# Two long attentions of a one-core kernel: which engine turns and splits the probabilities, where VectorE's side work stands, and how the softmax denominators are added

## What is computed

```python
x = x + xattn0(LN(x), ctx, mask)      # 16 heads of 64, 64 queries x 6272 keys, masked softmax   <- first long attention
x = x + attn0(LN(x))                  # 16 heads of 8 over the 64 tokens, rotary, causal
x = x + moe0(LN(x))                   # 8 experts of width 512, top 2
x = x + xattn1(LN(x), ctx)            # o1 = x1 + attn(x1, ctx); then attn(o1, o1, x1)            <- second long attention
x = x + delta1(LN(x))                 # gated delta rule with convolutions and FIR branches
x = x + ffn1(LN(x))                   # weights rounded to 8 bits per column, values to 16 bits
```

## Time and profile before

| | |
|---|---|
| median of three timed runs | 424.36 us |
| profiled execution, in all | 426.19 us |
| its span, first to last instruction | 424.4 us |
| mean granted TensorE clock | 0.984 |
| first long attention, first score to last PV | 22.0 to 177.2 us |
| second long attention | 217.8 to 365.4 us |
| DMA queue of SP | 186,080 packets, 66.31 MB |

### The profile page before, as it was taken

How to read it: one execution, slowest core, us unless ns; L and a number is a source line. 1 busy time by engine, 2 the same in 40 slices (tenths; PEclk the granted TensorE clock), 3 DMA queues, 4 the chain that set the end, 5 groups by cost and what they waited for, 6 DMA issues and landing times.

```text
span 424.4 us, 12031 instructions
## 1 busy us (share of the span) xinstructions
PE 390.8 (92%) x4785; PEld 309.7 (73%) x4785; DVE 317.9 (75%) x872; ACT 287.3 (68%) x568; POOL 203.1 (48%) x128
## 2 busy tenths in 40 slices
PE   6888999999989999998997899899999999999885
PEld 3846777777767778887964677677777778888784
DVE  2598888888877877645669999998888878454534
ACT  3367888788887886546427798789899876352230
POOL 2267879879865551001001559888766550020000
PEclk9699999999999999999999999999999999999969
DMA  8779797989989988960004999999999999400000
GB/s 318 297 219 172 151 175 126 181 137 207 239 165 231 213 164 141 405 280 2 4 2 88 197 169 193 189 172 182 188 204 198 194 192 237 175 2 3 4 0 5
DMA packets 186426, 68.14 MB, mean 161 GB/s; under 512 B 181361, under 2 KB 181889, under 8 KB 185473
## 3 DMA queue, kind: packets, MB, share of 16 engines
q1 hardware_dynamic: 186080, 66.31, 76.7%
q10 hardware_dynamic: 288, 1.05, 0.7%
HBM read 21.90 MB, written 0.03 MB: 52 GB/s over the span
## 4 chain that ended last, share of the span: by engine, by line
PE 44%; DVE 28%; issue 8%; DMA 6%; ACT 6%; POOL 4%; SPq 3%; DVEq 0%; POOLq 0%; ACTq 0%
PE ps L497 13%; DVE probs L591 12%; PE ps L465 12%; DMA probsT<-halves 4%; PE ps L725 4%; DVE probsT L620 3%; POOL halves L567 2%; ACT probs L535 2%; DVE U L609 2%; PE ps L1137 2%; PE ps L477 2%; PE ps L1042 2%; DMA moe<-in_ctxT 2%; DVE den L604 1%; ACT halves L542 1%
## 5 line engine op out<-in xcount | busy, mean ns | idle before, releaser
L567 POOL TENSOR_TENSOR halves<-probs,halves 128x896 f16<-128x896 f32 x67 | 126.6, 1892 | 81.9 <-ACT halves L542 81.1
L465 PE MATMUL ps<-ctxT_parts,GT_parts 128*128 128x512 f16 (+1 forms) x672 | 145.4, 353 | 11.9 <-DVE negmax L591 10.0
L497 PE MATMUL ps<-ctxN,probsT 128*128 128x128 f16 x2352 | 149.4, 219 | 5.0 <-DMA probsT<-halves 3.5
L497 PEld LDWEIGHTS ps<-ctxN,probsT 128*128 128x128 f16 x2352 | 139.6, 98 | 18.7 <-DVE U L609 4.9
L535 ACT ACTIVATE probs<-probs,shifted 128x896 f32<-128x896 f32 x112 | 115.5, 1031 | 9.7 <-DVE shifted L596 9.7
L465 PEld LDWEIGHTS ps<-ctxT_parts,GT_parts 128*128 128x128 f16 x672 | 60.0, 98 | 64.3 <-DVE negmax L591 14.9
L542 ACT CAST halves<-probs 128x896 f16<-128x896 f32 x92 | 84.9, 922 | 0.1
L591 DVE CUSTOM_DVE_ANT_0 probs<-ps,maskb,negmax 128x896 f32<-128x896 f32 x56 | 67.4, 1204 | 1.2 <-POOL halves L567 0.7
L591 DVE CUSTOM_DVE_ANT_0 probs<-ps,zero,negmax 128x896 f32<-128x896 f32 x56 | 67.4, 1204 | 1.0 <-PE ps L465 0.8
L609 DVE SCALAR_TENSOR_TENSOR U<-U,alpha,ps 128x128 f32<-128x128 f32 x112 | 38.2, 341 | 32.3 <-PE ps L497 32.3
L532 ACT ACTIVATE alpha<-negmax 128x1 f32<-128x1 f32 x96 | 28.2, 294 | 42.4 <-DVE negmax L591 41.5
(11 more groups left out here) (347 smaller groups left out, 361.0 us busy)
## 6 DMA issues: line engine op xcount, KB each, us to landing
moe<-in_ctxT SPq DMA_DIRECT2D x7, 448.0 KB, 8.0
moe<-in_mask SPq DMA_DIRECT2D x6, 448.0 KB, 10.7
moe<-in_gateT SPq DMA_DIRECT2D x2, 1024.0 KB, 9.3
moe<-in_upT SPq DMA_DIRECT2D x2, 1024.0 KB, 11.2
moe<-in_downT SPq DMA_DIRECT2D x2, 1024.0 KB, 13.1
moe<-in_fir_long SPq DMA_DIRECT2D x1, 2048.0 KB, 10.4
probsT<-halves SPq DMA_TRANSPOSE x92, 4.5
wv<-in_wv SPq DMA_DIRECT2D x2, 512.0 KB, 5.3
```

The source lines that it names most:

```text
L465: ins = pe.matmul(ps[:, 2 * b + h, 0:width], GT_parts[:, g_part, r * P:(r + 1) * P], ctxT_parts[:, keys:keys + width], start=(g_part == 0 ...
L497: ins = pe.matmul(ps[:, bank, 0:D], probsT_parts[:, b, p_part, k * P:(k + 1) * P], ctxN_parts[:, at:at + D], start=(p_part == 0 and c_part ...
L567: eng.tensor_tensor(halves_of(L, n)[:, 1, :], probs[:, n % BUFS, :], halves_of(L, n)[:, 0, :], ALU.subtract).then_inc(lower_of(L, n)[0], 1)
```

## The change

TensorE's turns in the first attention: before, every fourth step (n % 4 = 3) and 53 to 55; now n % 4 = 3 only for 4 <= n < 32, and 51, 53, 54, 55 as before. Step 3 goes to GpSimd and the DMA; steps 35, 39, 43 and 47 go to VectorE (low half) and the DMA. In the second attention VectorE no longer makes the low halves of steps 0, 1, 3, 7 and 11; GpSimd does. `den` is updated once per chunk for all eight row tiles with two instructions on 128 x 8 (behind the maximum of index 13, 21, 29, 37, 45 and 53); only the last chunk is still added column by column. The weight maxima stand behind the projection of the first attention and the scales in the small attention; `keep_o1` moves from index 2 to 14. The mask of chunk 1 is made one low half earlier, and the eight rounding stages stand at every fourth step from 12 to 40.

```diff
+TURN_UNTIL, RAMP = 32, 12
         def on_pe(L, n):
-            return L == 0 and n % 4 == 3 or n >= STEPS - 3 or n == STEPS - 5
+            return L == 0 and n % 4 == 3 and 4 <= n < TURN_UNTIL or n >= STEPS - 3 or n == STEPS - 5
         def on_vector(L, n):
             if L == 0:
-                return n in (0, 2) or 4 <= n < 30 and n % 4 == 1 or n == STEPS - 4
-            return n % 4 == 3 or n in (0, 1, STEPS - 4)
+                return (n in (0, 2) or 4 <= n < 30 and n % 4 == 1 or n >= TURN_UNTIL and n % 4 == 3
+                        or n == STEPS - 4)
+            return n >= RAMP and n % 4 == 3 or n == STEPS - 4
...
             def add(n):
-                r = n % RT
-                dve.wait_ge(sem("exp_done"), base + n + 1)
-                if n >= RT:
+                r, c = n % RT, n // RT
+                if c == CH - 1:
+                    dve.wait_ge(sem("exp_done"), base + n + 1)
                     dve.wait_ge(sem("den_added"), base + n - RT + 1)
-                dve.tensor_scalar(den[:, r:r + 1], den[:, r:r + 1], alpha[:, n:n + 1], chunksum[:, n:n + 1],
-                                  ALU.mult, ALU.add).then_inc(sem("den_added"), 1)
+                    dve.tensor_scalar(den[:, r:r + 1], den[:, r:r + 1], alpha[:, n:n + 1], chunksum[:, n:n + 1],
+                                      ALU.mult, ALU.add).then_inc(sem("den_added"), 1)
+                elif r == RT - 1:
+                    tiles = slice(c * RT, (c + 1) * RT)
+                    dve.wait_ge(sem("exp_done"), base + n + 1)
+                    if c:
+                        dve.wait_ge(sem("den_added"), base + c * RT)
+                    dve.tensor_tensor(den[:], den[:], alpha[:, tiles], ALU.mult).then_inc(sem("den_added"), 1)
+                    dve.wait_ge(sem("den_added"), base + c * RT + 1)
+                    dve.tensor_tensor(den[:], den[:], chunksum[:, tiles], ALU.add).then_inc(sem("den_added"), RT - 1)
...
-                if n == 2:
+                if n == 0:
                     mask(1)
...
-                        if 12 <= n < 28 and n % 2 == 0:
-                            quantise_weights((n - 12) // 8, (n - 12) // 2 % 4)
+                        if 12 <= n < 44 and n % 4 == 0:
+                            quantise_weights((n - 12) // 16, (n - 12) // 4 % 4)
...
             project_dve(dve, 0)
+            loaded(dve, "ffn")
+            for i, w in enumerate((win, wout)):
+                ins = dve.tensor_reduce(wamx[:, i * FT:(i + 1) * FT], w[:], AX, ALU.max, apply_absolute_value=True)
+            seq(ins)
             dve.wait_ge(sem("y_ready"), 1)
...
                                   ALU.mult).then_inc(sem("a_probs"), 1)
+            seq(dve.tensor_scalar(wamx[:], wamx[:], 1e-8, None, ALU.max))
+            seq(dve.reciprocal(wsc[:, 0, :], wamx[:]))
+            seq(dve.tensor_scalar(wsc[:, 0, :], wsc[:, 0, :], 127.0, None, ALU.mult))
+            dve.reciprocal(wsc[:, 1, :], wsc[:, 0, :]).then_inc(sem("f_scales"), 1)
             dve.wait_ge(sem("a_given"), A_GIVEN["out"])
...
-            flash_dve(dve, 1, {1: partial(g_lower_dve, dve, 1, slice(4 * P, 8 * P), 5), 2: keep_o1, 4: partial(weight_max, 0, win), 6: partial(weight_max, 1, wout),
-                               8: weight_scales, 20: residual_gate, 22: temperature})
+            flash_dve(dve, 1, {1: partial(g_lower_dve, dve, 1, slice(4 * P, 8 * P), 5), 14: keep_o1, 20: residual_gate,
+                               22: temperature})
```

More of the change, by code:

```diff
@@ L1633, in keep_o1 @@
                 seq(dve.tensor_tensor(x[:], x[:], W("bo"), ALU.add))
-            def weight_max(i, w):
-                loaded(dve, "ffn")
-                seq(dve.tensor_reduce(wamx[:, i * FT:(i + 1) * FT], w[:], AX, ALU.max, apply_absolute_value=True))
-            def weight_scales():
-                seq(dve.tensor_scalar(wamx[:], wamx[:], 1e-8, None, ALU.max))
-                seq(dve.reciprocal(wsc[:, 0, :], wamx[:]))
-                seq(dve.tensor_scalar(wsc[:, 0, :], wsc[:, 0, :], 127.0, None, ALU.mult))
-                dve.reciprocal(wsc[:, 1, :], wsc[:, 0, :]).then_inc(sem("f_scales"), 1)
             def residual_gate():
```

## The result

The changed kernel takes 427.04 us (median of 6 runs, 425.61 to 429.7) against 424.27: ratio 1.0067, 95% interval 1.0040 to 1.0094. It is slower; I had forecast 421.3. The profiled executions stand closer, 427.13 against 426.19, with spans of 425.3 and 424.4: the profiled run of before lay 1.8 us above its median, that of after on it. Part of this scatter arises before the first step. Over all kernels of this study VectorE's first maximum began 1.5 us earlier to 2.0 us later than in the trace of before, and TensorE's waits name loads of the inputs there (`wkT<-in_wkT` 2.2 us in the latest of them). TensorE's granted clock over the first 22 us goes with it: 0.92 in the five traces that began 1.2 to 1.5 us earlier, 0.84 in the kernel before, 0.77 in the changed kernel (0.6 us later) and 0.69 in the latest. So I compare stages by differences inside one trace.

The account below looks back on a forecast made before the run. TensorE, busy for 92% of the span, was taken as the bound. First attention -2.3 and second attention -0.8 gave -3.1 us, put on the median of 424.36: 421.3 us, range 416 to 428.

Parts of the forecast that it names:

- First attention from step 32: Steps 35, 39, 43, 47 lose TensorE's turn, SP issues four more transposes: 0 us, between -3.3 and +3.2.
- the second rival: SP's queue bounds the first attention from step 32, every transpose 1.98 us or more: +3.2, 424.5 us, chance 0.16.
- the bad end: Steps 33 to 50, first attention: nineteen transposes at 1.98 us, six loads and 24 pauses take 45.8 us, +3.2.
- The tail: Steps 51 to 55 of the first attention: as it was, no change.
- The best end: Steps 33 to 50 of the first attention: TensorE at its floor needs 39.3 us instead of 42.6, -3.3.
- Step 3 not turned: First attention, step 3 to GpSimd: only TensorE's own time goes, -0.9 us, between 0 and -2.1.
- Denominators, steps 4 to 31: First attention: seven groups without step-by-step `den` updates -2.7 us, three chunk additions +1.3.
- Ramp of the second attention: Steps 0 to 11: first PV at 231.3 instead of 233.40, seventh 14.2 us later, -3.8 us in all.
- Side work put back: Second attention, steps 12 to 46: chunk addition at 13 and `keep_o1` at 14 meet GpSimd work, +2.4 us.
- Later steps: Second attention: quantising over 32 steps and chunk additions on VectorE's chain, +0.6 us, between -1.5 and +2.
- Ports collide each time: Rival, both attentions: chunk pairs and `keep_o1` each wait one more whole GpSimd low half, 428 us, chance 0.28.

Follow-up runs that it names:

- e3: The changed kernel with `den` updated step by step again, as before: 429.96 us.
- e6: The changed kernel with TensorE's turns of the first attention back, `den` step by step and `keep_o1` at index 2: 421.15 us.
- e5: The changed kernel with `keep_o1` at index 2 of the second attention again: 425.52 us.
- e1: The changed kernel with TensorE turning steps 35, 39, 43 and 47 of the first attention again: 421.54 us.
- e11: e10, but steps 39 and 47 of the first attention not turned by TensorE, their transposes on the DMA: 419.23 us.
- e10: e8 with five weight loads issued behind the transpose of step 55: 418.65 us.
- e7: The changed kernel with five weight loads issued behind the transpose of step 55 instead of between those of steps 33 to 44: 423.44 us.
- e9: The changed kernel with DMA transposes of steps 33 to 50 of the first attention carrying half the bytes, part of the result left out: 416.42 us.
- e12: e11 with the weight loads back between the transposes, where the change has them: 421.97 us.
- e8: The changed kernel with TensorE's turns back, `keep_o1` at index 2, and chunk additions only in chunks 1 to 5 of the first attention: 419.60 us.
- e4: The kernel before with the second attention's part of the change alone, `den` step by step and `keep_o1` at 14: 425.60 us.

## Why the prediction was wrong

The step that failed is "First attention from step 32": I took 0 between -3.3 and +3.2, and it was +6.0 (steps 37 to 55). The mechanism stood in the text as the second rival, at 0.16 and at 424.5; its price was mis-sized.
- *The price per transpose.* I priced 19 transposes at 1.98 us as the bad end, a mean of a stretch in which SP still had room. The seventeen of steps 33 to 49 took 2.23 us on average in the changed kernel (the first and some of the last stand above), the two context transposes 1.6 and 3.25. That is (37.9 + 4.9) / 19 = 2.25 instead of 1.98, 5.1 us more; the loads took 5.2 us and not 6, and 45.8 became 50.4. The 0 that I took stood on twelve transposes at 1.98 and seven at 1.53, and on a further 1 us for which I gave no reason (the sum without it is 42.7, not 42.5). Six of the nineteen were short (1.5 us), so the count was nearly right; the other thirteen took 2.6 and not 1.98. A price read where the queue has pauses is no upper bound for a queue without any.
- *The tail.* "The tail (steps 51 to 55) is as it was" is wrong for VectorE's maximum: the lag grew by 2.6 us there, from 2.7 at step 50 to 5.3. The delay itself is older: SP issues the transpose of step 50 7.1 us later than in the kernel before (167.78 against 160.69) and that of step 52 5.3 later (170.18 against 164.91, where SP had paused for 2.7). A queue that is behind hands its delay on until something lets it catch up.
- The best end was right: with half the bytes steps 33 to 50 won 3.6 us, where TensorE's floor promised 3.3.

The other terms, by the same differences:
- *Step 3 not turned:* -0.9 forecast, -0.4 measured (start to step 8 in e3 and e6, where `den` is as before; 0.6 in the changed kernel): VectorE's low half of step 5, at 39.68, met GpSimd's context work and lasted 2.58 us instead of 1.22.
- *Denominators, steps 4 to 31:* -2.7 + 1.3 = -1.4 forecast, -0.5 measured (0.2 to step 8, 0.3 from there to step 31; e6 has the old updates and neither). The collisions were sized well. The chunk additions, and VectorE's low halves, with three of the GpSimd instructions they met, changed kernel:

```profile
55.23 1.68 POOL L1317 TENSOR_TENSOR moe<-moe,ch_scale 128x896 f32<-128x896 f32 x1
55.50 1.44 DVE L613 TENSOR_TENSOR den<-den,alpha 128x8 f32<-128x8 f32 x1
...
71.34 1.69 POOL L1317 TENSOR_TENSOR moe<-moe,ch_scale 128x896 f32<-128x896 f32 x1
72.09 1.89 DVE L569 TENSOR_TENSOR halves<-probs,halves 128x896 f16<-128x896 f32 x1
...
77.07 1.54 DVE L613 TENSOR_TENSOR den<-den,alpha 128x8 f32<-128x8 f32 x1
...
93.07 1.45 DVE L569 TENSOR_TENSOR halves<-probs,halves 128x896 f16<-128x896 f32 x1
...
97.20 3.22 POOL L1311 TENSOR_SCALAR maskb<-moe 128x896 bf16<-128x896 int32 x1
97.60 0.55 DVE L613 TENSOR_TENSOR den<-den,alpha 128x8 f32<-128x8 f32 x1
...
120.09 0.15 DVE L613 TENSOR_TENSOR den<-den,alpha 128x8 f32<-128x8 f32 x1
```

At indices 13, 21 and 29 they cost 0.9, 0.3 and 0.2 in steps (1.05, 0.25 and 0 forecast). Mis-sized was the gain: between two additions seven steps won 0.55, so a group of four won 0.3, not 0.38, and it began at index 6, with the first update left out. In the kernel before the same two low halves lasted less:

```profile
72.18 1.53 DVE L567 TENSOR_TENSOR halves<-probs,halves 128x896 f16<-128x896 f32 x1
...
93.41 1.08 DVE L567 TENSOR_TENSOR halves<-probs,halves 128x896 f16<-128x896 f32 x1
```

VectorE came earlier to them, GpSimd was not done, and they ended no earlier. So a part of what left VectorE's chain was taken back there. That this is the whole difference was not tested.
- *Ramp of the second attention:* the first PV was forecast at 231.3; it is at 236.62, which less the 5.3 us of lag is 231.3. The seventh came 14.6 us later where I had 14.2, so the ramp won 3.4 by then and not 3.8; 0.56 of the difference to the floor is the wait for a transpose. (VectorE's maximum, 4.7 better at step 10, is 3.4 better at step 13.) Changed kernel, first, fifth and seventh PV:

```profile
236.62 1.33 PE L499 MATMUL ps<-ctxN,probsT 128*128 128x128 f16 x21
...
246.57 1.33 PE L499 MATMUL ps<-ctxN,probsT 128*128 128x128 f16 x21 [0.56 <-DMA probsT<-halves]
...
251.18 1.34 PE L499 MATMUL ps<-ctxN,probsT 128*128 128x128 f16 x21
```

- *Side work put back:* +2.4 forecast, +2.5 measured at steps 13 to 15. The rule of the Trainium skill ("SBUF — State Buffer", section "Who interferes with whom"), that a VectorE instruction with two SBUF inputs contends with a GpSimd instruction that reads SBUF, on ports that are an exclusive lock, fits the trace: 1.76 us for a product of 128 x 8, to the end of GpSimd's low half. For the mask build it fits in part: the addition at 97.60 lasted 0.55 us beside it, not the 0.15 of 120.09, but did not wait for its 3.22. That section of the Trainium skill also names a one-input `tensor_scalar` in a two-port mode; `keep_o1`'s second instruction lasted 0.95 beside the quantising and 0.23 in e5.
- *Later steps:* +0.6 forecast, -2.0 measured (4.4 behind at step 15, 2.4 at step 55). Not taken apart here; e5, which loses 1.8 less before step 15, wins only 0.2 behind it, so the two may not be independent. The second attention won 2.9 instead of 0.8.

Added up on VectorE's maximum: -1.3 from the start to step 37, +6.0 from there to step 55, -2.9 in the second attention, together +1.8. With the start (+0.6) and the stretch behind the second attention (-1.5), which both go with the granted clock, that is the 0.9 us between the two spans.

The rival "Ports collide each time" had 428 and a chance of 0.28, and its number is near the result, but not its mechanism: of the chunk pairs only three met a GpSimd instruction for over a microsecond (55.50, 77.07, 254.14), and e5, without `keep_o1`'s collision, gets 1.5 us by the medians (2.8 by the ratios). What outweighed the gains was the queue: e1 alone gets 5.5 (6.4).

What stays open is how much of the difference of the medians (2.8, against 0.9 between the profiled executions and 1.8 without start and end) is scatter of the granted clock; and where the queue's limit lies: without the loads two more transposes win 0.4 us in the trace (e11 against e10) and four lose 3.2 (e7), and no run stands between.

## What to carry to other kernels

Work that leaves a busy engine for a DMA queue is priced at the rate of that queue when it is full, not at the rate read between its pauses; and its delay is followed to where the queue can catch up, past the stage that was changed. An instruction of VectorE that reads two SBUF operands is placed where GpSimd pauses, however small it is. Where two such meetings follow each other, taking one away can make the other longer, so they are judged together.

## What the runs showed of the hardware

- A DMA transpose of 128 x 1792 two-byte values took SP 1.53 us after most pauses of the queue (2.38 and 2.67 after the two longest of the kernel before), 2.23 on average in a queue without pauses, and one of half the size 1.22 to 1.60 (e9). The loads that SP issues in between took 0.57 to 1.11 us each there. On the end of the stage five of them cost 2.8 us beside four more transposes (e7), 2.4 beside two (e12) and 0.8 beside none (e10 against e8).
- The one-column `den` update (128 x 1, scalars by partition) lasted 0.27 us beside GpSimd's context multiplication, while `tensor_scalar` on 128 x 2 (the residual gate) lasted 1.07 in the changed kernel and ended with GpSimd's low half (271.39 to 273.28):

```profile
272.23 1.07 DVE L1655 TENSOR_SCALAR sres<-sres 128x2 f32<-128x2 f32 x1
```

- A wait of TensorE can cost more than its own time. After 3.19 us without work (e4) a group of scores took 2.42 us instead of 1.30, after 2.05 (e5) a PV took 2.40 instead of 1.33; the granted clock of these stretches is 0.72 (256 to 262 us) and 0.83 (150 to 160 us). In the changed kernel TensorE waited up to 2.3 us between 112 and 178 us, and the granted clock stayed at 1.00.
